# A graph and attention layer on one core: edges as one transfer, the low halves of the key and value weights on VectorE, one one-hot product on ScalarE, early query weight loads

## What is computed

```
xn = layernorm(x)
W = zeros(1024, 1024).at[src, dst].add(edge_weight)       # duplicates add up
graph = xn @ W.T + gnn_bias
q, k, v = split(xn @ W_qkv);  q, k = relu(rmsnorm(q, k))   # 16 heads of 64
kv = k^T v;  att = (q kv) / (q . sum(k) + eps)
x = x + graph + att @ W_out + b_out
t = rmsnorm(layernorm(x)) * norm_scale
x = x + sum over the top 2 of 8 experts of p * swiglu(t @ w1 + b1) @ w2 + b2
```

## Time and profile before

| | |
|---|---|
| runs, us | 1085.53, 1087.60, 1088.87, median 1087.6 |
| the profiled execution, us | 1086.58, its span 1084.7 |
| PE busy | 948.2 us, 87% |
| DVE busy | 731.1 us, 67% |
| ACT busy | 305.3 us, 28% |
| POOL busy | 186.7 us, 17% |
| mean granted clock of PE | 0.948 of full speed |

### The profile page before, as it was taken

One profiled execution on the slowest core, in us unless ns is written; L12 is line 12 of the kernel. 1 busy time (PEld: TensorE's weight loads), 2 busy tenths in 40 slices (PEclk: granted clock), 3 DMA queues, 4 the chain that ended last, 5 costly groups with the idle time before them and its releaser, 6 DMA issues.

```text
span 1084.7 us, 16241 instructions
## 1 busy us (share of the span) xinstructions
PE 948.2 (87%) x5425; PEld 589.6 (54%) x5426; DVE 731.1 (67%) x1213; ACT 305.3 (28%) x520; POOL 186.7 (17%) x217
## 2 busy tenths in 40 slices
PE   3589899888899599999999999997828999999992
PEld 2346566666566366545656666665615445455551
DVE  4646888999888599715787778765264555555551
ACT  3525333233333111423212222222102333233321
POOL 1210000000000000000334333322201333333321
PEclk9789899999999699999999999998858999999997
DMA  8512566555455601395115555555618997977553
GB/s 255 187 59 78 174 191 197 185 181 159 143 169 173 215 21 40 85 290 170 40 39 145 156 164 170 173 160 168 214 47 300 326 264 192 312 198 192 119 100 58
DMA packets 90410, 176.49 MB, mean 163 GB/s; under 512 B 25235, under 2 KB 40537, under 8 KB 90337
## 3 DMA queue, kind: packets, MB, share of 16 engines
q1 hardware_dynamic: 82577, 147.40, 42.6%
q0 software_dynamic: 7776, 28.32, 11.7%
HBM read 113.54 MB, written 62.67 MB: 162 GB/s over the span
## 4 chain that ended last, share of the span: by engine, by line
PE 35%; DVE 31%; DMA 14%; ACT 6%; issue 5%; POOL 4%; SPq 3%; DVEq 1%; POOLq 0%; ACTq 0%
PE windows L1066 9%; PE bank L943 8%; DMA arena<-t_dram,arena 6%; DMA arena<-in_w_flat 5%; PE bank L1084 4%; DVE arena L1476 4%; DVE arena L1483 3%; DVE arena L1630 3%; PE bank L966 2%; PE bank L790 2%; PE bank L1057 2%; PE bank L972 2%; POOL arena L687 2%; DVE arena L1463 2%; DVE arena L1461 2%
## 5 line engine op out<-in xcount | busy, mean ns | idle before, releaser
L790 PE MATMUL bank<-arena 128*125 128x512 f16 x960 | 222.5, 390 | 31.7 <-POOL arena L656 18.4
L790 PEld LDWEIGHTS bank<-arena 128*125 128x125 f16 x960 | 132.6, 141 | 109.4 <-issue 27.7
L1066 PE MATMUL windows<-arena 128*128 x648 | 148.8, 379 | 0.0
L943 PE MATMUL bank<-arena 128*128 128x416 f16 (+1 forms) x576 | 110.0, 348 | 9.4 <-DMA arena<-split_dram 9.4
L966 PE MATMUL bank<-arena 128*125 128x512 f16 x432 | 99.2, 387 | 8.3 <-DVE arena L1666 6.8
L1066 PEld LDWEIGHTS windows<-arena 128*128 128x128 f16 x648 | 63.4, 98 | 65.1 <-issue 0.5
L972 PE MATMUL bank<-arena 128*125 128x512 f16 x432 | 95.8, 379 | 0.0
L943 PEld LDWEIGHTS bank<-arena 128*128 128x128 f16 x576 | 56.3, 99 | 56.1 <-DMA arena<-split_dram 10.0
L966 PEld LDWEIGHTS bank<-arena 128*125 128x125 f16 x432 | 60.1, 140 | 43.8 <-DVE arena L1666 7.2
L972 PEld LDWEIGHTS bank<-arena 128*125 128x125 f16 x432 | 59.0, 137 | 33.4
L1084 PE MATMUL bank<-arena 128*128 x324 | 74.3, 379 | 2.2 <-DVE arena L1838 2.2
(11 more groups left out here) (243 smaller groups left out, 1453.5 us busy)
## 6 DMA issues: line engine op xcount, KB each, us to landing
arena<-split_dram SPq DMA_DIRECT2D x56, 512.0 KB, 7.0
arena<-in_w_flat SPq DMA_DIRECT2D x44, 512.0 KB, 4.7
split_dram<-arena SPq DMA_DIRECT2D x88, 256.0 KB, 2.7
arena<-in_w_flat SPq DMA_DIRECT2D x40, 256.0 KB, 3.3
split_dram<-arena SPq DMA_DIRECT2D x80, 128.0 KB, 2.3
arena<-in_x SPq DMA_DIRECT2D x20, 448.0 KB
arena<-in_w_qkv SPq DMA_DIRECT2D x8, 1024.0 KB, 9.5
t_dram<-arena SPq DMA_DIRECT2D x10, 448.0 KB
```

Of the source, the lines that this page charges most:

```text
L790: mm = pe.matmul(bank[b][0:TT, :], xt[:, l, k, tok(i)], wkv[:, r, k, c0:c0 + 512], start=(k == 0 and n == 0), stop=(k == KT - 1 and n == 2))
L943: mm = pe.matmul(bank[u % 3][:, 0:n], wq[h][:, l, k, :], xt[:, r, k, a:a + n], start=(k == 0 and c == 0), stop=(k == KT - 1 and c == 2))
L1066: mm = pe.matmul(bank[6][:, :], rowT[s][:, l, k, :], arena16[:, bass.ds(off + (r * KT + k) * 512, 512)], start=(k == 0 and c == 0), stop=( ...
```

## The change

Five edits, told in the order of the program.

1. The edges, with the fill values and the last two entries of each row before, are laid out on the host as one array of 128 rows of 1158 numbers, and come as one transfer. The four fills of POOL are gone.
2. DVE makes all 8 low halves of the key and value weights. The scaling in place on ACT and the three subtractions on POOL are gone. The third part is asked for at once. `window_counts` and `window_picks` stand later in DVE's list. Half pieces: `HALVES_OF` gives tile 1 six instead of four, tiles 8 and 9 four instead of five.
3. For groups 0 to 29 (`HOT_ON_ACT`) the product of keys and high weight moves from DVE to ACT, as 8 activations of 128 columns with the weight as a scale per row.
4. The first query weights are asked for before the pieces of tile 8, and PE computes the first query unit ahead of the last `kv_sums`.
5. The quarters per tile are 6, 5, 5, 5, 5, 5, 5, 4 instead of 5, 5, 5, 5, 6, 6, 4, 4, and in the last two tiles `add_half` stands behind the third and the fourth quarter on DVE.

```diff
+HOT_ON_ACT = KV_GROUPS - 2
-        LO_ON_POOL = (3, 5, 7)
-        HALVES_OF = [0, 4] + [5] * (NT - 2)
+        HALVES_OF = [0, 6, 5, 5, 5, 5, 5, 5, 4, 4]
-        QUARTERS_OF = {2: 5, 3: 5, 4: 5, 5: 5, 6: 6, 7: 6, 8: 4, 9: 4}
+        QUARTERS_OF = {2: 6, 3: 5, 4: 5, 5: 5, 6: 5, 7: 5, 8: 5, 9: 4}
...
+            load_wkv(2)
             load_x(1)
+            sp.dma_start(edges_all, edges).then_inc(table_in, 16)
             sp.dma_start(knw, kn_w.partition_broadcast(P)).then_inc(knw_in, 16)
-            load_wkv(2)
             load_wkv(3)
+            load_wkv(4)
             load_x(2)
-            load_wkv(4)
+            load_wkv(5)
             load_x(3)
-            for m in (5, 6, 7):
+            for m in (6, 7):
                 load_wkv(m)
...
             for i in range(NT):
                 for n in halves(i):
+                    if n == 2 * EARLY - 1:
+                        sp.wait_ge(kv_mm, 4 * NT)
+                        load_wq(0, 1)
                     store(n)
...
+                if i == NT - 3:
+                    for h in range(2):
+                        sp.wait_ge(part_out[h], 32 * N_PIECE_Q)
+                    load_wq(0, 0)
...
-            pe.wait_ge(v_lo, 2 * NT)
-            kv_sums()
...
                     mm.then_inc(q_mm, 1)
+                    if first and u == 0:
+                        pe.wait_ge(v_lo, 2 * NT)
+                        kv_sums()
...
+            def hot_scale(n):
+                pairs_of = one_hot[n % 2][:, 1, :].rearrange("p (a k j) -> p a k j", a=G // 2, j=2)
+                a_.wait_ge(hot_key, 2 * n + 2)
+                for j in range(G):
+                    col = pairs_of[:, j // 2, :, j % 2]
+                    ins = a_.activation(col, col, ACT.Copy, scale=whi[:, n * G + j:n * G + j + 1])
+                ins.then_inc(hot_ready, 1)
...
             for i in range(2, NT):
                 n, hs = 4 * (i - 2), halves(i)
                 k_half(i, 0)
                 piece_hi(hs[0])
+                if n + 2 < HOT_ON_ACT:
+                    hot_scale(n + 2)
                 k_half(i, 1)
                 k_root(i)
+                piece_hi(hs[1])
                 if i + 1 < NT:
                     xt_hi_half(i + 1, 0)
-                piece_hi(hs[1])
+                if n + 3 < HOT_ON_ACT:
+                    hot_scale(n + 3)
                 a_.wait_ge(k_rs, i + 1)
                 v_half(i, 0)
                 piece_hi(hs[2])
-                if i + 2 < NT:
-                    ln_sqrt(i + 2)
                 if i + 1 < NT:
                     xt_hi_half(i + 1, 1)
                 piece_hi(hs[3])
+                if n + 4 < HOT_ON_ACT:
+                    hot_scale(n + 4)
+                if i + 2 < NT:
+                    ln_sqrt(i + 2)
                 v_half(i, 1)
-                piece_hi(hs[4])
+                for m in hs[4:]:
+                    piece_hi(m)
+                if n + 5 < HOT_ON_ACT:
+                    hot_scale(n + 5)
...
                 v.tensor_tensor(pairs_of(one_hot[s][:, 2, :]), key_hot, cols(wlo), ALU.mult).then_inc(hot_key, 1)
-                v.wait_ge(hot_key, 2 * n + 2)
-                v.tensor_tensor(key_hot, key_hot, cols(whi), ALU.mult).then_inc(hot_ready, 1)
+                if n >= HOT_ON_ACT:
+                    v.wait_ge(hot_key, 2 * n + 2)
+                    v.tensor_tensor(key_hot, key_hot, cols(whi16), ALU.mult).then_inc(hot_ready, 1)
...
-                for q in quarters(i):
+                for q in quarters(i, 0, 3):
                     quarter_split(q)
-                for half in range(2):
-                    add_half(i, i % 2, half)
+                add_half(i, i % 2, 0)
+                for q in quarters(i, 3, 4):
+                    quarter_split(q)
+                add_half(i, i % 2, 1)
```

More of the change, by code:

```diff
@@ L485, in _ @@
             ask(1)
-            for i in range(NT):
-                for n in halves(i):
-                    store(n)
-                    if n + 2 < 2 * EARLY:
-                        ask(n + 2)
-                if i + 5 < NT:
-                    load_x(i + 5)
             def load_wq(t, h):
@@ L1505, in _ @@
             wkv_part_lo(0)
[L1506 removed]
             for half in range(2):
                 xt_lo_half(0, half)
+            wkv_part_lo(1)
+            stats(1)
+            wkv_part_lo(2)
+            norm(1)
             window_counts()
[L1510 to L1514 removed]
+            for m in (3, 4):
+                wkv_part_lo(m)
             v.wait_ge(knw_in, 16)
             k_half(0, 0)
[L1517 removed]
+            for m in (5, 6):
+                wkv_part_lo(m)
             k_half(0, 1)
+            wkv_part_lo(7)
             norm_of_k(0)
@@ L1525, in _ @@
                 v_half(0, c)
+            window_picks()
+            hs = halves(1)
+            for n in hs[0:2]:
+                piece_lo(n)
             v.wait_ge(kv_used, START + 1)
@@ L1572, in _ @@
                 accumulate(n + 3)
-                piece_lo(hs[4])
+                for m in hs[4:]:
+                    piece_lo(m)
             v.wait_ge(qn_in, 16)
```

156 lines of the change are left out of this document (71 added, 85 removed).

## The result

The changed kernel takes 1092.32 us (median of 6 runs, 1091.83 to 1094.32), the kernel before 1085.98 beside it. The ratio is 1.0059, with a 95% interval of 1.0042 to 1.0077: slower by some 6 us, more than the 0.3% that can be told from no change. The forecast was 1083.9, a little faster. The value lies inside the range of 1067 to 1099, but the sign is wrong.

The account below looks back on a forecast made before the run. In the loop PE and DVE both look full, with DVE setting the pace. The terms -9.8 + 25.3 - 11.5 - 6.7 gave -2.7 us against 1086.6, so 1083.9 us, eight in ten from 1067 to 1099.

Parts of the forecast that it names:

- mixing term: Mixing, edit 5: moved quarters let PE start the last tile earlier and without its clock loss, -6.7 us.
- One more in tile 2 and one less in tile 6 cancel: Mixing: an extra quarter at a tile's end costs about 2.5 us, so these two moves net to nothing.
- Start: Start to tile 2, edits 1 and 2: weights go out earlier, tile 2 starts at 101.2, -9.8 us.
- Rival 4: Start: weights arrive later or DVE becomes the bound; half of the 9.8 us is gone, 1089; chance 0.10.
- Loop: Loop over the tiles, edit 3: 35.7 us per tile against 31.9, +25.3 us.
- H: Loop: time of ACT's eight activations per group, taken as 2.53 us, bounded by 1.7 and 3.2.
- Rivals 1 and 2: Loop: H near 1.7 us, 18 us shorter, 1066, chance 0.15; or H 3.2, 15 us longer, 1099, chance 0.15.
- Rival 3: Loop: PE, idle more, loses its clock and sets the pace at 38.3 us per tile, +18, 1102; chance 0.05.
- Its answers to DVE now stand behind the eight activations: Loop: ACT works in order, so DVE waits behind H three times per tile, 28.15 + 3H = 35.7 us.
- To the queries: Last value half to first query addition, edit 4: 7.9 us instead of 19.2, -11.5 us.

Follow-up runs that it names:

- d1: Kernel before with its edge weights padded by 97,896 bytes, no instruction changed: 1087.0 us, ratio 1.0005.
- e2: Kernel before with the flat weights declared as first input, no instruction changed: 1084.4 us, ratio 0.9972.
- a4: Kernel before with edit 5 alone (new table of quarters, moved additions in the last two tiles): 1083.0 us, ratio 0.9955.
- a2: Changed kernel with the old table of quarters, additions of the last two tiles left as changed: 1100.6 us, ratio 1.0110.
- b4: Changed kernel with the edge tensor declared last instead of second, no instruction changed: 1086.6 us, ratio 0.9997 to the kernel before.
- d2: Changed kernel with the flat weights declared first instead of seventh, no instruction changed: 1079.7 us, ratio 0.9922 to the kernel before.
- a3: Changed kernel with SP asking for the third quarter before it waits for POOL's sum and stores it: 1086.6 us, ratio 0.9988 to the kernel before.
- b3: Kernel before with edit 5 and the single edge tensor of edit 1: 1083.6 us, ratio 0.9980.
- b1: Changed kernel with each batch of eight activations put behind ACT's next answer to DVE: 1054.9 us, ratio 0.9691 to the kernel before.
- c1: Changed kernel with edit 4 undone: 1100.1 us, ratio 1.0140 to the kernel before.
- a1: Changed kernel with edit 3 undone, the product back on DVE in every group: 1067.9 us, ratio 0.9828 to the kernel before.
- c4: Changed kernel with the eight clearings of the sums moved from ACT to POOL: 1092.3 us, ratio 1.0056 to the kernel before.

## Why the prediction was wrong

**The step that failed is in the mixing term: "One more in tile 2 and one less in tile 6 cancel".** Tiles 2 to 6 should have come out even and cost 5.3 us. Tiles 7 to 9 gave 6.2 us, against the forecast's 6.7, and by the forecast's mechanism: PE starts the last tile without its long wait and at full clock. Their size is partly luck: d1 and e2 have the mixing instructions of the kernel before, and against them the gain is 4 us. The rounds added up, in us:

| kernel | table of quarters, inputs | tiles 2 to 6 | tiles 7 to 9 |
|---|---|---|---|
| before, d1, e2 | old, no edge tensor | 131.5, 131.6, 131.4 | 70.5, 68.4, 68.1 |
| a4 | new, no edge tensor | 134.8 | 62.3 |
| a2 | old, edge tensor second | 137.4 | 68.6 |
| after | new, edge tensor second | 136.8 | 64.3 |
| b4, d2 | new, other orders | 133.6, 133.2 | 61.1, 61.5 |
| a3 | as after, early request | 130.0 | 61.5 |

Either of two things lengthens tiles 2 to 6. Edit 5 alone costs 3.3 us (a4): with the sixth quarter in tile 2 the rounds behind no longer come down to 24.9 us but stay at 26.4 to 26.9 in tiles 4 to 6. The new list of inputs costs 3.3 to 3.6 (after against b4 and d2). They don't add up, and the exchange of quarters by itself is not what fails in the changed kernel, since with the old table (a2) it takes no less, 137.4. What the forecast lacked, as I read these sums, is a term for the round itself: it priced a quarter where it stands, and not the way from DVE's norm over SP's list to the third quarter, which holds a round at some 26.7 us as soon as PE's lead is used up or the quarters land later. a3, which shortens that way alone, brings rounds 4 to 6 to 24.7 and the five tiles to 130.0. That the same way paces a4 is argued from the length of its rounds and was not tried. The forecast also priced edit 1 by the issues that leave SP's queue, and did not see that a new list of inputs can change how fast later transfers land. What stays open: the property of the place that does it. The round of 24.9 us in tile 5 before is scatter in part: d1 and e2 read 25.3 and 25.9 there.

**Start: -7.5 instead of -9.8.** The term was too large by 2.4 us. PE's last unit of tile 0 began at 48.09 (forecast 47.5). From there to tile 2 it took 55.5 us, not 53.7: the square stands behind the activations and six clearings, as forecast, and so does the value half of tile 1, which waited for PE. Over all profiled kernels with edits 1 and 2 tile 2 started between 102.0 and 107.3. b3 suggests that edit 1 alone gives 4.0 us here; edit 2 was not tried alone. Rival 4, that the start does not gain, was wrong, and its remark that one transfer does nothing too.

**Loop: +25.7 against +25.3.** H measured 2.48 us against 2.53, the three steps of a tile 8.76, 9.96 and 16.7 (forecast 8.93, 10.02, 16.79). Rivals 1 and 2, on H, are decided: neighbours with a scale per row overlap. Rival 3 did not set the pace: the granted clock over the loop fell from 0.98 to 0.95 and PE was busy for 214.8 us instead of 200.9, but that fitted into its idle time. "Its answers to DVE now stand behind the eight activations" was the right cause: b1 takes the whole term away by turning that round.

**To the queries: -12.0 against -11.5.** The sum was right by luck: by c1 only 5.6 us of it are edit 4's, and the rest, put down to edit 4 as well, came from another edit.

With 2.4 us more at the start and 5.8 in mixing the forecast of -2.7 becomes +5.5, against 5.7 in the span and 6.3 by the medians. Of the Trainium skill ("ScalarE: Activation LUTs", What ACT_TABLE_LOAD costs) the figures were borne out for the batch: the estimate of H worked out from them, 2.44 us, lies 0.04 under the 2.48 measured. The skill's rule in the same page (Rules for kernel authors), that a product belongs on VectorE, fits the list as it was changed (a1 is faster), but not the one in b1, where ACT has the time.

## What to carry to other kernels

Before pricing work that moves to another engine, look at what stands behind it in that engine's list: an answer that somebody waits for must come first, the bulk after it. The same eight activations cost 26 us ahead of the answers and gave 14 behind them, and a request in SP's list behind a foreign wait cost 6 to 9. When work is handed out to stages, price the round that repeats (who asks, who waits, when it lands), and not only the piece that moves. A change in the list of inputs is part of a change: run it with another order of inputs before judging an effect under 1%. Here the same instructions read 0.6% slower, equal or 0.8% faster than the kernel before (after, b4, d2).

## What the runs showed of the hardware

- The same transfers of 256 KB from the flat weights land in 3.2, 3.5 or 4.1 us (medians) by the order in which the inputs are declared, with no instruction changed (after 4.1, b4 3.2, d2 3.5); padding by 62 and 98 KB had no effect, and in the kernel before the order moved them from 3.3 to 3.4 only (e2). Each figure is from one profile; the eight profiled kernels with the edge tensor second and SP's old list read 4.0 to 4.3. With the request ahead of POOL's sum they land in 3.9 to 4.5 us in any order. I had no such term.
- Eight activations on 128x128 with a scale per row, on columns four bytes apart, take 2.47 to 2.49 us, one alone 424 ns by the trace: so they start 0.29 us apart.
- POOL cleared 128x1024 f32 eight times in 7.16 us (c4), no slower than ACT, which took 5.77 for six.
- The unchanged kernel's own runs on one chip spread over 1.2%; edits of a few us had to be read from marks in the trace, which scatter as well (mixing by 2.5 us over three profiles of the same instructions).
